# Five row buffers in an expert block, and another order and bank for the last item's gate sums

## What is computed

```python
x = x + jnp.tanh(g_xattn[0]) * _L0_xattn_ref(_layernorm(x), ctx, mask, ...)   # cross attention, 16 heads
x = x + jnp.tanh(g_ffn[0])   * _L0_ffn_ref(_layernorm(x), ...)                # top 2 of 8 experts
x = x + jnp.tanh(g_xattn[1]) * _L1_xattn_ref(_layernorm(x), ctx, ctx)
x = x + jnp.tanh(g_ffn[1])   * _L1_ffn_ref(_layernorm(x), ...)                # 8 groups, low-rank mixing

def _L0_ffn_ref(x, rw1, rw2, w1, b1, w2, b2):
    probs = softmax(gelu(x @ rw1) @ rw2)
    wgt, idx = top_k(probs, 2)
    for e in range(8):
        Ye = gelu(x @ w1[e] + b1[e]) @ w2[e] + b2[e]
        ...                        # out += wgt * Ye where token and slot chose e

def _fused_linear(x, W, qa, qb, scale, w):       # _L1_ffn_ref uses it for gate, up and down
    out = x @ W.T
    a = einsum('th,krh->tkr', x, qa)
    b = einsum('tkr,khr->tkh', a, qb)
    return out + scale * einsum('tkh,tk->th', b, w)

def expert(...):                                  # for each of 8 groups f
    xe = x + w @ muW.T
    gate = silu(_fused_linear(xe, gW, gqa, gqb, gs, w))
    up = _fused_linear(xe, uW, uqa, uqb, us, w)
    return _fused_linear(gate * up, dW, dqa, dqb, ds, w)
```

## Time and profile before

| | us |
|---|---|
| median of 3 runs | 630.34 (630.17 to 630.4) |
| profiled execution | 629.24 |
| its span on the core | 627.5 |
| PE busy | 586.2 (93%) |
| DVE busy | 472.8 (75%) |
| ACT busy | 345.0 (55%) |
| POOL busy | 263.3 (42%) |

### The profile page before, as it was taken

How to read it: one execution, slowest core, us unless ns; L and a number is a source line. 1 busy time by engine, 2 the same in 40 slices (tenths; PEclk the granted TensorE clock), 3 DMA queues, 4 the chain that set the end, 5 groups by cost and what they waited for, 6 DMA issues and landing times. The chain is left out here.

```text
span 627.5 us, 12397 instructions
## 1 busy us (share of the span) xinstructions
PE 586.2 (93%) x4384; PEld 478.6 (76%) x4384; DVE 472.8 (75%) x858; ACT 345.0 (55%) x617; POOL 263.3 (42%) x282
## 2 busy tenths in 40 slices
PE   6989899999899999999799979999999999999995
PEld 3567667899899999999545667886777877777774
DVE  4468365887787777685669878968888888888954
ACT  2535035395687677575468765655454456455540
POOL 4331410682253253344268323077457446465300
PEclk9999998999999999999999999999999999999997
DMA  8098640778988787765041030052230330311002
GB/s 255 25 330 238 198 149 2 264 266 266 305 237 218 199 235 193 228 176 160 10 134 46 14 103 1 1 148 50 85 98 0 98 96 3 97 43 56 0 2 67
DMA packets 59332, 79.90 MB, mean 127 GB/s; under 512 B 7008, under 2 KB 51376, under 8 KB 58160
## 3 DMA queue, kind: packets, MB, share of 16 engines
q1 hardware_dynamic: 53952, 72.60, 36.8%
q0 software_dynamic: 4224, 5.26, 4.5%
q10 hardware_dynamic: 1104, 1.35, 0.6%
HBM read 66.23 MB, written 11.58 MB: 124 GB/s over the span
## 5 line engine op out<-in xcount | busy, mean ns | idle before, releaser
L1068 POOL DMA_INDIRECT moe_sum<-yb,xs x24 | 52.8, 2199 | 88.5 <-ACT yb L1270 70.6
L1962 POOL TENSOR_TENSOR wlo<-raw,whi 128x352 fp32r<-128x352 f32 (+1 forms) x48 | 56.8, 1215 | 43.1 <-DVE hlo L2232 24.8
L1141 PE MATMUL bank<-xhi,wlo 128*128 128x256 f32 (+1 forms) x240 | 67.2, 280 | 1.0 <-issue 1.0
L1141 PE MATMUL bank<-xhi,whi 128*128 128x256 f32 (+1 forms) x240 | 67.4, 281 | 0.0
L1141 PE MATMUL bank<-xlo,whi 128*128 128x256 f32 (+1 forms) x240 | 67.4, 281 | 0.0
L1160 PE MATMUL bank<-whi,hlo 128*128 128x256 f32 x208 | 59.1, 284 | 0.0
L1160 PE MATMUL bank<-whi,hhi 128*128 128x256 f32 x208 | 58.0, 279 | 0.0
L1160 PE MATMUL bank<-wlo,hhi 128*128 128x256 f32 x208 | 58.0, 279 | 0.0
L2485 PE MATMUL bank<-nhi,wlo 128*128 128x512 f32 x128 | 52.5, 410 | 0.6 <-PEq L2111 0.4
L2485 PE MATMUL bank<-nhi,whi 128*128 128x512 f32 x128 | 50.4, 394 | 0.0
L2485 PE MATMUL bank<-nlo,whi 128*128 128x512 f32 x128 | 50.3, 393 | 0.0
(11 more groups left out here) (426 smaller groups left out, 1720.2 us busy)
## 6 DMA issues: line engine op xcount, KB each, us to landing
raw<-w_in SPq DMA_DIRECT2D x19, 1024.0 KB, 7.9
rawb<-w_in SPq DMA_DIRECT2D x14, 1024.0 KB, 6.8
raw<-wf_in SPq DMA_DIRECT2D x8, 1088.0 KB
moe_rows<-zrow SPq DMA_DIRECT2D x10, 387.0 KB, 6.4
xs<-moe_rows SPq DMA_DIRECT2D x11, 258.0 KB, 3.1
scb<-sc_in SPq DMA_DIRECT2D x16, 160.0 KB
cv<-ctx_in SPq DMA_DIRECT2D x32, 64.0 KB, 2.1
moe_sum<-zrow SPq DMA_DIRECT2D x1, 1280.0 KB, 7.4
```

Of the source, the lines that this page charges most:

```text
L1068: nc.gpsimd.indirect_dma_start(xacc, bass.IndirectOffsetOnAxis(ap=xs[:, i % 4, t, D:D + 1].bitcast(I32), axis=0), yb[:, i % 2, t, :], None ...
L1141: last = nc.tensor.matmul(psum[b][:, half:half + tiles_of(i) * P], w[:, s, at:at + P], a[:, s, k, 0:tiles_of(i) * P], start=(n == 0), stop ...
L1962: nc.gpsimd.tensor_tensor(wlo[:, s, a:b], raw[:, a:b], whi[:, s, a:b].bitcast(F32), ALU.subtract).then_inc(prep_ready if b == WN else prep ...
```

## The change

1. `xs` has five places (`RING = 5`) and as many semaphores, and every index `i % 4` and count `i // 4` of it becomes `i % RING` and `i // RING`. `tokens(i)` waits from i = 5 on, for item i-5.
2. In the last call of the last stage `dq` goes to bank 2 (`dq_bank`), and PE waits there neither for the four x of item 14 ahead of `dq` nor for `wadf_ready` ahead of the first output.
3. DVE's additions for item 14: in the call for item 15 tile 0 is not added between h0f and h1f any more; tiles 0 and 1 are added after the low parts h0lo and h1lo. In the last call tile 2 is added ahead of h1f from `dq`, tile 3 behind it.

```diff
+            RING = 5
...
-            xs = buf("xs", [P, 4, 2, XW], F32, s4)
+            xs = buf("xs", [P, RING, 2, XW], F32, s4)
...
                     def tokens(i):
-                        if i >= 4:
-                            sp.wait_ge(y_added, 16 * tiles_before(i - 3))
+                        if i >= RING:
+                            sp.wait_ge(y_added, 16 * tiles_before(i - RING + 1))
...
-                        sp.dma_start(xs[:, i % 4, 0:n, :],
+                        sp.dma_start(xs[:, i % RING, 0:n, :],
...
+                def dq_bank(i):
+
+                    return 7 if i is not None else 2
...
                                 wait(pe, "hlo_ready", 2 * prev["n"] + 2)
-                                if i is None:
-                                    wait(pe, "acc_ready", TC * prev["n"])
                                 sp_, cp = prev["s"], prev["c"]
...
-                                split_product(psum[7][:, :], terms, True, True).then_inc(q8["dq_done"], 1)
+                                split_product(psum[dq_bank(i)][:, :], terms, True, True).then_inc(q8["dq_done"], 1)
...
-                                wait(pe, "wadf_ready", m + 1)
+                                if i is not None:
+                                    wait(pe, "wadf_ready", m + 1)
                                 wait(pe, "acc_ready", TC * (m - 1) + 1)
                                 output(0, 0)
...
                                 m, cp = prev["n"], prev["c"]
+                                if i is None:
+                                    accumulate(before_last, [2])
                                 wait(dve, "dq_done", m + 1)
-                                nc.vector.tensor_tensor(h1f[UB:P, :], psum[7][UB:P, :], we[UB:P, cp, :], ALU.mult
+                                nc.vector.tensor_tensor(h1f[UB:P, :], psum[dq_bank(i)][UB:P, :], we[UB:P, cp, :], ALU.mult
                                                         ).then_inc(q8["wadf_ready"], 1)
+                                if i is None:
+                                    accumulate(before_last, [3])
                                 wait(dve, "wadhi_ready", m + 1)
...
-                            if prev is not None:
+                            if prev is not None and (i is None or nxt is not None):
                                 accumulate(prev, [0])
...
                             if prev is not None and nxt is None:
-                                accumulate(prev, range(1, TC))
-
+                                accumulate(prev, [0, 1] if i is not None else range(1, TC))
+
+                        before_last = item_of(G1 - 1, 1, NCH - 2)
```

More of the change, by code:

```diff
@@ L940, in build @@
             w1_in_sem, w2_in_sem = [sem4(f"w1_in{s}") for s in range(2)], [sem4(f"w2_in{s}") for s in range(2)]
-            xs_in, b1_sem = [sem4(f"xs_in{s}") for s in range(4)], [sem4(f"b1_in{s}") for s in range(4)]
+            xs_in, b1_sem = [sem4(f"xs_in{s}") for s in range(RING)], [sem4(f"b1_in{s}") for s in range(4)]
             placed, w1b_in, copied, take_ready = sem("placed"), sem4("w1b_in"), sem4("hx_copied"), sem4("take_ready")
@@ L1000, in tokens @@
                     def tokens(i):
-                        if i >= 4:
-                            sp.wait_ge(y_added, 16 * tiles_before(i - 3))
+                        if i >= RING:
+                            sp.wait_ge(y_added, 16 * tiles_before(i - RING + 1))
                         n = tiles_of(i)
-                        sp.dma_start(xs[:, i % 4, 0:n, :],
+                        sp.dma_start(xs[:, i % RING, 0:n, :],
                                      xg[ST * i:ST * i + n * P, :].rearrange("(t p) d -> p t d", p=P)
-                                     ).then_inc(xs_in[i % 4], 16)
+                                     ).then_inc(xs_in[i % RING], 16)
                     sp.wait_ge(routing_ready, 1)
@@ L1062, in _ @@
                     for i in range(NSLOT - 2):
-                        pool.wait_ge(xs_in[i % 4], 16 * (i // 4 + 1))
+                        pool.wait_ge(xs_in[i % RING], 16 * (i // RING + 1))
                         if i:
@@ L1068, in _ @@
                             nc.gpsimd.indirect_dma_start(xacc, bass.IndirectOffsetOnAxis(
-                                ap=xs[:, i % 4, t, D:D + 1].bitcast(I32), axis=0), yb[:, i % 2, t, :], None,
+                                ap=xs[:, i % RING, t, D:D + 1].bitcast(I32), axis=0), yb[:, i % 2, t, :], None,
                                 compute_op=ALU.add).then_inc(y_added, 16)
@@ L1117, in turn @@
                     def turn(i):
-                        pe.wait_ge(xs_in[i % 4], 16 * (i // 4 + 1))
+                        pe.wait_ge(xs_in[i % RING], 16 * (i // RING + 1))
                         pe.wait_ge(xlo_ready, i - 1)
@@ L1123, in turn @@
                                 last = nc.tensor.transpose(turn_bank(i)[:, at:at + P],
-                                                           xs[:, i % 4, t, k * P:(k + 1) * P], ident[:, :])
+                                                           xs[:, i % RING, t, k * P:(k + 1) * P], ident[:, :])
                         last.then_inc(x_turned, 1)
@@ L1264, in y_out @@
                         s = i % 2
-                        act.wait_ge(xs_in[i % 4], 16 * (i // 4 + 1))
+                        act.wait_ge(xs_in[i % RING], 16 * (i // RING + 1))
                         act.wait_ge(y_done, i + 1)
@@ L1270, in y_out @@
                             nc.scalar.activation(yb[:, s, t, :], y_bank(i)[:, t * D:(t + 1) * D], ACT.Copy,
-                                                 scale=xs[:, i % 4, t, D + 1:D + 2]).then_inc(y_ready, 1)
+                                                 scale=xs[:, i % RING, t, D + 1:D + 2]).then_inc(y_ready, 1)
                     def first_high(part, arrived):
@@ L1302, in y_high @@
                         nc.scalar.activation(xhi[:, i % 2, :, P:2 * P], by_k(y_bank(i)[:, 0:D]), ACT.Copy,
-                                             scale=xs[:, i % 4, 0, D + 1:D + 2]).then_inc(yhi_ready, 1)
+                                             scale=xs[:, i % RING, 0, D + 1:D + 2]).then_inc(yhi_ready, 1)
                     y_high(NSLOT - 2)
@@ L1523, in last_places @@
                         i = NSLOT - 2 + n
-                        dve.wait_ge(xs_in[i % 4], 16 * (i // 4 + 1))
-                        v(nc.vector.tensor_copy(lastf[:, n, 0:1], xs[:, i % 4, 0, D:D + 1].bitcast(I32)))
+                        dve.wait_ge(xs_in[i % RING], 16 * (i // RING + 1))
+                        v(nc.vector.tensor_copy(lastf[:, n, 0:1], xs[:, i % RING, 0, D:D + 1].bitcast(I32)))
                         v.wait()
@@ L1571, in y_low @@
                         nc.vector.scalar_tensor_tensor(xlo[:, i % 2, :, P:2 * P], by_k(y_bank(i)[:, 0:D]),
-                                                       xs[:, i % 4, 0, D + 1:D + 2], xhi[:, i % 2, :, P:2 * P].bitcast(F32),
+                                                       xs[:, i % RING, 0, D + 1:D + 2], xhi[:, i % 2, :, P:2 * P].bitcast(F32),
                                                        ALU.mult, ALU.subtract).then_inc(ylo_ready, 1)
```

## The result

| | before | after |
|---|---|---|
| median, same chip (22 runs each) | 630.72 | 626.54 |
| profiled execution's span | 627.5 | 624.9 |
| DVE's h0f of item 15 to the end of the last x | 14.65 | 9.06 |

The changed kernel took 0.9908 of the time of the kernel before, 95% interval 0.9887 to 0.9929: 4.5 to 7.1 us less, 5.8 at the middle. This ratio leaves out the slow executions, five of the 22 after among them (630.4 us and more), and with all 22 of each kernel the medians lie 4.2 us apart and the means 5.0. The forecast was 6.0 less than a base of 630.34, which gave 624.3.

What follows compares the result with a forecast made beforehand. PE was taken as the bound, so gains come only where it idles or its clock is low. Terms 2.94 + 1.22 + 1.67 = 5.8 us, with 0.2 for the rows 6.0, took 630.34 to 624.3; range 622.7 to 627.5.

Steps and rivals of the forecast that it cites:

- Part 1, rows of item 4: Expert block: the fifth buffer lets tokens(4) go out 4.5 us sooner, but in a full queue gains 0.2 us (0 to 1.7).
- from item 5 on rows that come sooner buy nothing: Expert block: later turns have no bracket and PE needs 11.83 us an item, so sooner rows gain nothing.
- `dq` 2.94 sooner: Last item: PE starts dq at about 613.33 instead of 616.27, a gain of 2.94 us.
- From `dq` to h1f: Last item: with no gap the clock stays up, so 2.81 us becomes 1.59, a gain of 1.22.
- From h1lo to the first x: Last item: PE issues most first-half products earlier, so 2.26 us becomes 0.59, a gain of 1.67.
- wrong if `dq` starts after 614: Sign against the forecast: in the changed kernel's PE timeline, the last item's dq starting later than 614 us.
- the first x near 617.6: Sign for the forecast: in the changed kernel's timeline the first x of item 15 comes near 617.6 us.
- The clock as the profile's alone: Rival, 0.14: timed executions lack the slow clock behind the gap, so only 2.94 plus 0.2 us is gained; 627.2 us.
- 1.3 us: Whole kernel: about 0.2%, taken as what a measurement can tell from no change.
- Rows sooner: Rival, 0.10: each DMA engine has room, so the fifth buffer gives 1.7 us instead of 0.2; 622.8 us.
- The order that does not hold: Rival, 0.05: at the end h1lo is late by another path and the gain is below 1.3 us; 629 to 630.3.
- Stores of y as the bound: Rival, 0.03: expert block's accumulating store pairs average over 11.83 us and delay later loads; 631.6 us or more.

Runs made afterwards that it cites:

- e1: The kernel before with five row buffers (RING = 5) and the last stage unchanged; 633.51 us, ratio 0.997 to the kernel before.
- e11: The changed kernel with the rows of item 4 requested ahead of the second matrix of item 4; 622.78 us, ratio 0.9891 to the kernel before.
- e2: The changed kernel with four row buffers instead of five, keeping the new bank and order at the end; 629.29 us, ratio 0.9933 to the kernel before.
- e7: The kernel before with 12 calls of products nobody reads, put in PE's gap ahead of the last dq; 627.3 us, ratio 0.9876 to the kernel before.
- e5: The changed kernel with four row buffers and DVE's old order, so only dq's bank and PE's waits are new; 625.76 us, ratio 0.9845 to the kernel before.
- e10: The changed kernel with four row buffers and 16 unused bytes between xs and xhi; 624.42 us, ratio 0.9922 to the kernel before.
- e6: The changed kernel with four row buffers, bank 7 and PE's old waits; DVE adds item 14's four tiles behind the low parts; 630.7 us, ratio 0.9955 to the kernel before.
- e9: The changed kernel with four row buffers used but five places allocated for xs; 626.27 us, ratio 0.9936 to the kernel before.
- e4: The changed kernel itself, run again without edits; 628.47 us, ratio 0.9881 to the kernel before.
- e3: The changed kernel with the rows of item 4 requested ahead of the second matrix of item 4, first run; 628.27 us, ratio 0.9867 to the kernel before.

## Why the prediction was right, step by step

*Part 1, rows of item 4.* The bracket before `turn(4)` stayed (2.42, and 2.57 in e1, against 2.17) with the request at 157.55, near the 156 given. e1's ratio allows 4.1 us less to 0.3 us more, and the term was 0.2 less, so the timed runs neither confirm nor refute it; the bracket does. The Trainium skill, "DMA: Bandwidth & Descriptors", section "Queues, rings and completion order", has each DMA engine take its descriptors in order; the constant 17.9 us and the rows of e11, at 13.6 instead of 17.8, agree.

*Part 1, "from item 5 on rows that come sooner buy nothing".* Right for the rows, wrong for what is queued behind them. I named `first_matrix(i+1)` behind the wait and then priced only the rows. That is where e2 got its gap and its ten slow microseconds. And the ten items from `turn(4)` to `turn(14)` do run faster with five buffers, 112.8 us (e1) instead of 113.7, by the place of xhi and xlo, which no step had. Of this 0.9 us nothing arrives at `far_r`. Behind the items ACT waits in both kernels for the same load (before, then e1):

```profile
295.68 1.27 ACT L1313 ACTIVATE whi<-raw 128x1280 fp32r<-128x1280 f32 x1 [4.88 <-DMA raw<-ws_in]
```

```profile
295.37 1.27 ACT L1314 ACTIVATE whi<-raw 128x1280 fp32r<-128x1280 f32 x1 [6.13 <-DMA raw<-ws_in]
```

`turn(14)` was at 277.92 in the one and 276.24 in the other, 1.7 us apart; here they are 0.3 apart. From `turn(4)` to `far_r` it is 147.9 us before and 148.3 in e1. So the profiles don't show the term of 0.2 as a gain, and that it did no harm to the forecast is in part luck: it stands for effects of either sign that I had not seen.

*The end, term by term.* From h0f(15): `dq` 2.94 sooner forecast, 2.92 measured (5.84 to 2.92). From `dq` to h1f 1.22 less forecast, 1.11 measured (2.81 to 1.70). From h1lo to the first x 1.67 less forecast, 1.55 measured (2.26 to 0.71). h1f to h1lo 2.08 in both. Sum 5.8 forecast, 5.6 measured. The brackets that I expected next on PE, 0.3 and 0.6 us, are 0.26 and 0.25, the second less than half. The first x of item 15 came at 620.87 instead of 617.6; 3.0 of that lies ahead of h0f. So the sign "wrong if `dq` starts after 614" was badly put, and so was "the first x near 617.6": `dq` started at 616.38 although the step is right. A mark should be given from a neighbouring instruction, not from the span's start.

*The rivals.* The clock as the profile's alone (0.14) falls with the result, since it left a gain of 3.1 us, below the 4.5 to 7.1 measured, and with e7: with only filler in the gap the timed executions got shorter by 1.2% (0.6 to 1.9) and their granted clock rose, though by more than the profile's 2.7 us (0.4%). My argument against this rival was worth nothing: that three runs agreed within 0.23 us was chance, since 22 of the same kernel spread over 11.9. For the same reason 1.3 us was too small a limit of what can be told from no change, as 22 runs each give an interval 2.6 us wide. And the rule beside the rival has some truth. The Trainium skill, "TensorE: Matmul & The Clock Gate", section "Part 1: The HAM clock gate", says the gate's timing is not tied to the kernel's start. Single gaps of PE in these profiles agree: those of 1.66 (e5), 1.84 (e10), 2.17 (before) and 2.57 us (e1) kept the clock, those of 1.92 (e6), 2.34 (e9), 2.42 (after) and 3.05 us (before) lost it, the 3.05 of e1 for only half as long as that of before. The clearest pairs are 2.43 (e7, kept) with 2.42 (after, lost), both before `turn(4)`, and the two of e6. Length alone didn't decide among gaps of about 2 us. Rows sooner (0.10) falls with e1, but e11 shows that sooner rows were to be had by the order. The order that does not hold falls with the table of ends. Stores of y as the bound (0.03): the kernel got faster, and after `turn(4)` no `turn` of it waits for rows.

## What to carry to other kernels

A request moved ahead in time but not past anything in its queue is only a longer wait; to bring data sooner, look at what stands ahead of it, and price every request behind the wait that is removed, not only the one with the wait. A gap of PE near 2 us costs itself (e5) or, in other cases that its length didn't tell apart, itself and as much or more again in slow products (e6, 2.5 us behind a gap of 1.92): fill it with products that nobody reads (e7) if it can't be closed. Before a small gain is put down to an edit, compare the time of one product in unchanged loops: an added buffer moves its neighbours in SBUF.

## What the runs showed of the hardware that I had not expected

*The place of operands in SBUF.* The same product of 256 columns at 2.4 GHz started every 117.2 to 121.5 ns on the mean of its loop, and 16 bytes of distance between buffers were enough to move it by about 2 ns.

*Where some of the spread comes from.* Nine of the 14 profiles have, in `hidden(0)`, a bracket of about a microsecond with no releaser, the kernel before one of 1.02 us. In e4 there are six, 0.17 to 1.32 us (timeline of PE, then windows):

```profile
128.50 0.36 PE L1142 MATMUL bank<-xlo,whi 128*128 128x256 f32 x1 [0.96 <-issue]
...
132.03 0.37 PE L1142 MATMUL bank<-xhi,wlo 128*128 128x256 f32 x1 [1.32 <-issue]
...
134.15 0.58 PE L1142 MATMUL bank<-xhi,whi 128*128 128x256 f32 x1 [1.03 <-issue]
```

```profile
127.00:130.00 3.00, 1.10 (x6) 0.87 (x6) 0.85 (x3) 1.52 (x2) 2.18 (x3) 0.95 1.09 381
130.00:136.00 6.00, 3.31 (x12) 2.62 (x12) 5.00 (x6) 1.86 (x4) 5.23 (x3) 0.50 0.90 345
```

PE waits for nothing that the profile names while the DMA engines are full (share 1.09), and then runs at 1.2 GHz until 139.9. From the first mark to `turn(4)` e4 took 54.6 us, the profile of the same kernel above 51.5. e3 has ten such brackets and took 58.8, e11, the same kernel, 48.0. So such a row of stalls is worth 3 us and more. It stands in two of 14 profiles; the timed executions don't show it, but the five longest of the changed kernel (630.4 to 636.4 us) have a mean granted clock of 0.973 to 0.986 and the five shortest (620.8 to 622.9) 0.991 to 0.995. What PE lacks there stays open. Its own instructions, brought by the same DMA engines, were a guess, and the trace gives it no support: the DMA record of e4 has no packet of instructions in 126 to 136, and one, of 0.02 MB, in 136 to 139, when the six stalls are over. A request that still stood in a queue would leave no packet, so the guess isn't excluded either. With such a spread a single profile, or a median of three runs, could not have measured a change of 6 us.
